# A selective scan on one core: four of sixteen states get their input through ScalarE and TensorE, GpSimd takes one more pair of products

## The chip, the cores and the metric

One of the cores of a Trainium2 chip runs the whole program. The time is the device time of one execution in microseconds (us); lower is better. TensorE does the matmuls and transposes, VectorE (DVE in the rows) the scans, ScalarE (ACT) the exponentials and copies, GpSimd (POOL) elementwise products, SyncE (SP) issues most DMAs.

## The reference, cut to what matters

A Mamba-style layer (inner width 1024, 16 states) over 4 sequences of 1024 tokens, followed by a routed transformer block on 128 chosen tokens of each sequence. All is float32. The change touches the recurrence alone, for each channel `e`, state `n` and token `t`:

```
dA[n]    = exp(delta * A[n])
state[n] = state[n] * dA[n] + (delta * u) * B[n]
y        = sum over n of state[n] * C[n]
y        = (y + D * u) * silu(z)
x        = x + tanh(g) * y      (turned: tokens by channels)
```

`delta` and `u` are channels by tokens; `B[n]` and `C[n]` are rows over the tokens, the same for all channels.

## The kernel before, in words

The program runs in stages: a projection, the **first scan** (sequences 0 and 1), routing and the transformer block for them, the **second scan** (sequences 2 and 3), routing and block again. Both scans are `scan_stage`. A scan works through 32 **units** (`UNITS`): 2 sequences, 2 halves of 512 tokens, 8 tiles of 128 channels. A unit is 128 channels by 512 tokens with 16 states, in 8 pairs. Eight units in a row share one half, and so B and C. The second half of a sequence starts its scans from `carry`; the first half ends by saving it (L820, L825, a short ScalarE copy for each pair). I call these *first-half* and *second-half* units.

For each unit `s`:
- GpSimd makes delta and `du` = delta * u of the next unit (`begin`, L592 and L596) and `x[n]` = du * B[n] for four states at once (`quad`, L607).
- ScalarE makes dA of each state with an Exp into one of four PSUM banks `pA[n % 4]` (L903). It goes pair by pair: `release(s, i - 2)` first waits until the pair that used the two banks before is done with. Between the exps it does other pieces: the softplus of the next unit, the copy of the turned gate (`copy_gate`, L798), copies for the early or late side work. I call pair `i` with what follows it on ScalarE **slot** `i`.
- VectorE scans (L969): in0 the bank, in1 `x[n]`, out in the bank, or in `hp` for the two pairs (2 and 5) whose product with C GpSimd makes (L614). The products of the other six pairs are VectorE's (L954). Its order is scan `2i`, product of pair `i-1`, scan `2i+1`. The gate multiply (L943) of the unit before stands in slot 2.
- TensorE turns each product and adds it up in `py` (4 transposes a state, `add_state`, L670), pair by pair in `SUM_ORDER`. It also runs `dt_proj` (L642), the turning of the gate (L651) and, after the gate multiply, adds x to the result in PSUM (`add_x`, L659 and L660), which ScalarE copies out (L806). One PSUM bank `pm` serves all of these in turn.

Every engine takes its instructions strictly in the order written; semaphores make it wait.

Beside this, TensorE carries other work, put after given positions of the sum order. The first scan holds a projection and convolution for the later sequences (L723, L734). The second holds an MLP of the first half's chosen tokens (`feed_forward`): 25 steps a unit, dealt out to the eight positions by `FILL`; its activations are cut into ScalarE's slots (L831 to L841) and VectorE's (L975, L982, L987), 48 VectorE instructions in all.

Behind `store(s - 1)` on SP, which waits for the finished x of the unit before, stand some loads of B and C (`load_B(c, 3)`, `load_C(c, 1)`) at a change of the half.

## Time and profile before

| | us |
|---|---|
| median of three runs | 3032.66 (3030.67 to 3033.72) |
| the profiled execution | 3037.04 |
| its span, first to last instruction | 3035.3 |
| first scan, from first to last VectorE scan | about 189 to 1026 |
| second scan | about 1432 to 2310 |

The span is 1.7 us short of the profiled execution, and that one is 4.4 us over the median. Over the whole span TensorE is busy for 79%, VectorE for 70%, GpSimd for 55% and ScalarE for 44%, but these are averages over stages of quite different kinds. In both scans VectorE is the one near full.

### The profile page before, as it was taken

The numbers are of one execution on the slowest core, as the hardware profiler recorded it, in microseconds if no ns is written. First come the engines' busy times: TensorE is split into PE (matmuls) and PEld (weight loads), VectorE is DVE, ScalarE is ACT, GpSimd is POOL, SyncE is SP. The second block draws the span as 40 slices with busy tenths as digits, with TensorE's granted clock in tenths as the row PEclk, the third lists the DMA queues.
The fourth block names the chain that finished last, engine by engine and source line by source line (L and its number), as shares of the span: only waits on it lengthen the run. The fifth ranks groups of instructions, "written<-read, shape, count | busy, mean of one in ns | idle before, by whom it ended". The sixth has DMA issues, their size and how long they took to land. (4 is left out here: it accounts for less than half of the span.)

```text
span 3035.3 us, 30042 instructions
## 1 busy us (share of the span) xinstructions
PE 2390.7 (79%) x10552; PEld 1599.8 (53%) x10552; DVE 2112.7 (70%) x2626; ACT 1339.2 (44%) x2470; POOL 1667.7 (55%) x600
## 2 busy tenths in 40 slices
PE   8848767777777546887888888888884199999998
PEld 3324444444444316653666666664552186668863
DVE  6759999999999763232999999999997633310000
ACT  5647755666555341042665555565552212410000
POOL 1169999999999400002998998999993100000000
PEclk9959999999888857998999999999997599999999
DMA  9942252342522394624235335336333453145443
GB/s 335 334 140 78 65 167 77 108 143 63 159 70 60 126 359 143 229 78 142 84 104 187 105 104 175 118 97 215 97 108 133 186 179 104 46 141 153 153 152 104
DMA packets 224869, 426.70 MB, mean 141 GB/s; under 512 B 17488, under 2 KB 101712, under 8 KB 221904
## 3 DMA queue, kind: packets, MB, share of 16 engines
q1 hardware_dynamic: 211216, 368.68, 38.6%
q10 hardware_dynamic: 12160, 51.39, 4.2%
q0 software_dynamic: 1344, 4.72, 0.4%
q8 instruction: 85, 1.39, 0.2%
q14 instruction: 64, 0.52, 0.1%
HBM read 340.84 MB, written 83.89 MB: 140 GB/s over the span
## 5 line engine op out<-in xcount | busy, mean ns | idle before, releaser
L607 POOL TENSOR_TENSOR s_x<-s_du,k_bB 128x2048 f32<-128x2048 f32 x256 | 1156.4, 4534 | 82.8 <-PE s_py L670 52.7
L903 ACT ACTIVATE s_pA<-s_delta,k_negA 128x512 f32<-128x512 f32 x1024 | 664.1, 680 | 382.3 <-DVE s_x L954 373.5
L670 PE MATMUL s_py<-k_ident,s_x 128*128 128x128 f32 x4096 | 581.8, 289 | 254.8 <-DVE s_x L954 243.6
L670 PEld LDWEIGHTS s_py<-k_ident,s_x 128*128 128x128 f32 x4096 | 506.9, 150 | 479.9 <-DVE s_x L954 331.8
L969 DVE TENSOR_TENSOR_SCAN s_pA<-s_pA,s_x 128x512 f32<-128x512 f32 x384 | 452.2, 1214 | 63.5 <-POOL s_x L607 60.7
L954 DVE TENSOR_TENSOR s_x<-s_pA,k_bC 128x1024 f32<-128x1024 f32 x384 | 464.4, 1209 | 20.6 <-DMA k_bC<-scratch_xd 20.6
L969 DVE TENSOR_TENSOR_SCAN s_pA<-s_pA,s_carry,s_x 128x512 f32<-128x512 f32 x384 | 472.8, 1276 | 3.3 <-ACT s_pA L903 1.8
L1543 PE MATMUL l_p<-l_hT,l_ring 128*128 128x256 f32 x1792 | 397.4, 381 | 2.5 <-DVE l_hT L1736 1.4
L1543 PEld LDWEIGHTS l_p<-l_hT,l_ring 128*128 128x128 f32 x1792 | 342.2, 191 | 50.4 <-issue 2.0
L614 POOL TENSOR_TENSOR s_x<-s_hp,k_bC 128x1024 f32<-128x1024 f32 x128 | 302.0, 2359 | 16.4 <-DVE s_hp L969 16.1
L1511 POOL TENSOR_TENSOR l_squares<-l_squares,l_minus_half 128x1 f32<-128x1 f32 x4 | 2.2, 556 | 508.0 <-DVE l_squares L1802 508.0
L1550 PE MATMUL l_p<-l_ring,l_hidden 128*128 128x512 f32 x512 | 220.2, 592 | 0.0
L1520 POOL DMA_INDIRECT out_dram<-l_rows,l_row_i x2 | 1.9, 953 | 331.1 <-DVE l_rows L1829 331.1
L820 ACT ACTIVATE s_carry<-s_pA 128x2 f32<-128x2 f32 x192 | 33.0, 172 | 303.2 <-DVE s_x L954 302.5
L969 DVE TENSOR_TENSOR_SCAN s_hp<-s_pA,s_carry,s_x 128x512 f32<-128x512 f32 x128 | 162.6, 1271 | 0.0
L1550 PEld LDWEIGHTS l_p<-l_ring,l_hidden 128*128 128x128 f32 x512 | 97.1, 190 | 121.1 <-issue 121.0
L1824 DVE TENSOR_TENSOR l_hidden<-l_silu,l_p 128x256 f32<-128x256 f32 x32 | 13.5, 421 | 208.4 <-PE l_p L1543 208.4
L969 DVE TENSOR_TENSOR_SCAN s_hp<-s_pA,s_x 128x512 f32<-128x512 f32 x128 | 154.5, 1207 | 0.2 <-issue 0.2
L659 PE MATMUL s_pm<-s_xt,k_ident 128*128 128x512 f32 x128 | 77.9, 693 | 96.6 <-DVE s_gy L943 90.7
L734 PE MATMUL s_p_conv<-s_raw,s_diagC 128*128 128x512 f32 x256 | 148.5, 667 | 0.9 <-ACT s_pre L884 0.9
L686 PE MATMUL s_p_gate<-s_h2T,s_ring 128*128 128x256 f32 x512 | 138.1, 407 | 0.0
L723 PE MATMUL s_p_in<-s_ctxT,s_w_in 128*128 128x512 f32 x256 | 132.7, 600 | 0.0
(194 smaller groups left out, 3086.2 us busy)
## 6 DMA issues: line engine op xcount, KB each, us to landing
k_bB<-scratch_xd SPq DMA_DIRECT2D x32, 1024.0 KB, 12.1
k_bC<-scratch_xd SPq DMA_DIRECT2D x32, 1024.0 KB, 13.3
p_xz<-in_x SPq DMA_DIRECT2D x32, 512.0 KB, 6.6
scratch_ug<-p_ug ACTq DMA_DIRECT2D x16, 1024.0 KB, 8.7
k_u<-scratch_ug SPq DMA_DIRECT2D x64, 256.0 KB, 3.6
s_gy<-scratch_ug SPq DMA_DIRECT2D x64, 256.0 KB, 4.3
s_xt<-in_x SPq DMA_DIRECT2D x64, 256.0 KB, 4.7
scratch_x<-s_xt SPq DMA_DIRECT2D x64, 256.0 KB, 3.5
```

The source lines that it names most:

```text
L607: pool.tensor_tensor(out=x[:, 4 * g:4 * g + 4], in0=du[:, s % 2:s % 2 + 1].broadcast_to([P, 4, HALF]), in1=bB[:, 4 * g:4 * g + 4], op=ALU. ...
L614: pool.tensor_tensor(out=x[:, 2 * i:2 * i + 2], in0=hp[:, POOL_PAIRS.index(i)], in1=bC[:, 2 * i:2 * i + 2], op=ALU.mult).then_inc(pool_hc, 1)
L659: nc.tensor.matmul(pm[:], ident[:], xt[:, s % 3], start=True, stop=False)
L670: last = nc.tensor.matmul(py[:, a], x[:, n, a * P:(a + 1) * P], ident[:], is_transpose=True, start=False, stop=is_last and a == HALF // P - 1)
L686: last = nc.tensor.matmul(out[:, m % 2 * ROWS:(m % 2 + 1) * ROWS], ring[:, tile % RING, c * P:(c + 1) * P], h2T[:, c], start=r % (2 * KT) ...
L723: last = nc.tensor.matmul(p_in[:], w_in[:, s % 2, i], ctxT[:, chunk(s) % 2, i], start=i == 0, stop=i == NK - 1)
L734: last = nc.tensor.matmul(p_conv[:], diagC[:, s % NE, i], raw[:, s % 2, i:i + HALF], start=i == 0, stop=i == TAPS - 1)
L903: nc.scalar.activation(pA[:, n % 4], delta[:, s % 2], ACT.Exp, scale=negA[:, s % NE, n:n + 1]).then_inc(dA_ready, 1)
L954: nc.vector.tensor_tensor(x[:, 2 * i:2 * i + 2], pA[:, j:j + 2], bC[:, 2 * i:2 * i + 2], ALU.mult).then_inc(vec_hc, 1)
L969: nc.vector.tensor_tensor_scan(out, pA[:, n % 4], x[:, n], initial, ALU.mult, ALU.add).then_inc(scanned, 1)
L1543: last = nc.tensor.matmul(out[:, 0:ROWS], w[:, c * P:(c + 1) * P], src[:, c], start=c == 0, stop=c == KT - 1)
L1550: last = nc.tensor.matmul(banks[2 * a + h][:], src[:, a * P:(a + 1) * P], w[:, h * HALF:(h + 1) * HALF], start=is_first, stop=is_last)
```

## The change: four states in turned layout, one pair more for GpSimd

Pairs 3 and 7 (states 6, 7, 14, 15) are **turned** pairs. Their `x[n]` comes another way. TensorE turns `du` of the next unit into `pm` (`turn_du`, 4 transposes), ScalarE copies it out (`copy_du`), makes du-turned times B for each of the four states in four pieces of 128 by 128, with B as a column scale (`make_state`), and TensorE turns each back into the bank `pA[n % 4]` (`turn_x`, 4 transposes a state). The exps of these pairs go to SBUF, into `x[n]`, and the scan reads the two with their parts swapped. The columns of B are loaded by `load_columns`, one element of 4 bytes at a time in both patterns.

GpSimd makes two quads of four and two of two, takes three pairs times C (1, 3 and 5; VectorE keeps five) and adds x to the result itself (`add_x`), after `quad(s + 1, 1)`. TensorE's two `add_x` matmuls and ScalarE's copy go. Positions move: the gate is turned after the first sum (before: after the fourth) and copied in slot 5 (before: 7); `FILL` still has 25 steps, nine of them now after the third sum.

The core of the diff:

```diff
-POOL_PAIRS = (2, 5)
+POOL_PAIRS = (1, 3, 5)
+TURNED = (3, 7)
-SUM_ORDER = (0, 1, 3, 2, 4, 6, 5, 7)
+SUM_ORDER = (0, 1, 2, 4, 3, 5, 6, 7)
-GATE_AT, TURN_AT, DT_AT = 2, 3, 6
-READ_AT, X2_AT, COPY_AT = 2, 5, 7
+GATE_AT, TURN_AT, DU_AT, DT_AT = 2, 0, 2, 5
+READ_AT, COPY_AT, DU_COPY_AT = 1, 5, 6
+STATE_AT = (6, 7, 4, 5)
-FILL = (2, 2, 3, 3, 3, 3, 4, 5)
+FILL = (1, 3, 9, 1, 1, 3, 3, 4)
...
+    def load_columns(self, sp, t, b, th, j, sem):
+        for k, n in enumerate((6, 7, 14, 15)):
+            at = b * ND + NR + n
+            sp.dma_start(self.BT[:, j, k], t["xd"][at:at + 1, th * HALF:(th + 1) * HALF].rearrange("n (a p) -> p (n a)", p=P),
+                         allow_slow_non_contiguous=True).then_inc(sem, 16)
...
+            def add_x(s):
+                pool.wait_ge(y_used, s + 1)
+                pool.wait_ge(xt_in[s % 3], ring3(s)[1])
+                pool.tensor_tensor(out=xt[:, s % 3], in0=xt[:, s % 3], in1=gy[:, s % 3], op=ALU.add).then_inc(x2_ready, 1)
...
+            def turn_du(s):
+                pe.wait_ge(du_ready, s + 1)
+                if s:
+                    pe.wait_ge(gate_turned, s)
+                for a in range(HALF // P):
+                    last = nc.tensor.transpose(pm[:, a * P:(a + 1) * P], du[:, s % 2, a * P:(a + 1) * P], ident[:])
+                last.then_inc(du_turned, 1)
+
+            def turn_x(s, i):
+                pe.wait_ge(scanned, NS * s + 2 * i - 2)
+                for n in (2 * i, 2 * i + 1):
+                    k = state_at(0, n) - 1
+                    pe.wait_ge(xT_ready, state_at(s, n))
+                    for a in range(HALF // P):
+                        last = nc.tensor.transpose(pA[:, n % 4, a * P:(a + 1) * P], xT[:, k, a * P:(a + 1) * P], ident[:])
+                    last.then_inc(x_turned, 1)
...
+                turn_x(s, TURNED[0])
...
+                    if i == TURNED[1] - 3:
+                        turn_x(s, TURNED[1])
                     if at == TURN_AT:
                         turn_gate(s)
+                    if at == DU_AT and s + 1 < UNITS:
+                        turn_du(s + 1)
...
+            def copy_du(s):
+                act.wait_ge(du_turned, s + 1)
+                act.wait_ge(xT_ready, NT * s)
+                nc.scalar.activation(duT[:], pm[:], ACT.Copy).then_inc(duT_ready, 1)
+
+            def make_state(s, k):
...
+                for a in range(HALF // P):
+                    last = nc.scalar.activation(xT[:, k, a * P:(a + 1) * P], duT[:, a * P:(a + 1) * P], ACT.Copy,
+                                                scale=BT[:, chunk(s) % 2, k, a:a + 1])
...
-                nc.vector.tensor_tensor_scan(out, pA[:, n % 4], x[:, n], initial, ALU.mult, ALU.add).then_inc(scanned, 1)
+                dA, added = pA[:, n % 4], x[:, n]
+                if i in TURNED:
+                    dve.wait_ge(x_turned, state_at(s, n))
+                    dA, added = added, dA
+                nc.vector.tensor_tensor_scan(out, dA, added, initial, ALU.mult, ALU.add).then_inc(scanned, 1)
```

ScalarE in the first scan, the second half of a unit. Before, from the exps of pair 4 on (L903 exps, L806 copy of x, L798 copy of the gate, L802 the scaling of u for the next unit):

```order
L903 ACTIVATE s_pA<-s_delta,k_negA 128x512 x2
L806 ACTIVATE s_xt<-s_pm 128x512
L903 ACTIVATE s_pA<-s_delta,k_negA 128x512 x4
L798 ACTIVATE s_gy<-s_pm,k_tg 128x512
L903 ACTIVATE s_pA<-s_delta,k_negA 128x512 x2
L802 ACTIVATE k_u<-k_u,k_ssm 128x512
```

And now the same stretch, slots 4 to 7 and the next unit's first exps (L966 exps, L861 `make_state`, L840 gate, L849 `copy_du`, L844 u):

```order
L966 ACTIVATE s_pA<-s_delta,k_negA 128x512 x2
L861 ACTIVATE s_xT<-s_duT,k_BT 128x128 x4
L966 ACTIVATE s_pA<-s_delta,k_negA 128x512 x2
L840 ACTIVATE s_gy<-s_pm,k_tg 128x512
L861 ACTIVATE s_xT<-s_duT,k_BT 128x128 x4
L966 ACTIVATE s_pA<-s_delta,k_negA 128x512 x2
L849 ACTIVATE s_duT<-s_pm 128x512
L861 ACTIVATE s_xT<-s_duT,k_BT 128x128 x4
L966 ACTIVATE s_x<-s_delta,k_negA 128x512 x2
L861 ACTIVATE s_xT<-s_duT,k_BT 128x128 x4
L966 ACTIVATE s_pA<-s_delta,k_negA 128x512 x2
L844 ACTIVATE k_u<-k_u,k_ssm 128x512
```

Each of slots 4 to 7 now carries one state's four pieces, and the gate's copy has moved from slot 7 to slot 5.

TensorE in the second scan, the middle of a unit. Before, from the sum of pair 1 (L670 sums, L686 MLP steps, L651 turning of the gate):

```order
L670 MATMUL s_py<-k_ident,s_x 128x128 x8
L686 MATMUL s_p_up<-s_h2T,s_ring 128x256 x2
L670 MATMUL s_py<-k_ident,s_x 128x128 x8
L686 MATMUL s_p_up<-s_h2T,s_ring 128x256 x3
L670 MATMUL s_py<-k_ident,s_x 128x128 x8
L651 MATMUL s_pm<-k_ident,s_gy 128x128 x4
L686 MATMUL s_p_up<-s_h2T,s_ring 128x256 x3
L670 MATMUL s_py<-k_ident,s_x 128x128 x8
```

And now, from the unit's start (L697 `turn_x`, L702 u, L708 sums, L680 gate, L724 MLP steps, L688 `turn_du`):

```order
L697 MATMUL s_pA<-k_ident,s_xT 128x128 x8
L702 MATMUL s_py<-k_ident,k_u 128x128 x4
L708 MATMUL s_py<-k_ident,s_x 128x128 x8
L680 MATMUL s_pm<-k_ident,s_gy 128x128 x4
L724 MATMUL s_p_up<-s_h2T,s_ring 128x256
L708 MATMUL s_py<-k_ident,s_x 128x128 x8
L724 MATMUL s_p_up<-s_h2T,s_ring 128x256 x3
L708 MATMUL s_py<-k_ident,s_x 128x128 x8
L688 MATMUL s_pm<-k_ident,s_du 128x128 x4
L724 MATMUL s_p_up<-s_h2T,s_ring 128x256 x9
L708 MATMUL s_py<-k_ident,s_x 128x128 x8
L697 MATMUL s_pA<-k_ident,s_xT 128x128 x8
```

After the third sum (pair 2) stand the four transposes of `du`, nine MLP steps, the sum of pair 4, and only then the transposes that scans 14 and 15 read.

## Rows read from the trace of the kernel before

**Rows 1.** The page, the span in 40 slices: VectorE's busy tenths.

```profile
DVE  6759999999999763232999999999997633310000
```

**Rows 2.** Timeline of VectorE, first scan, a first-half unit: start, duration, instruction.

```profile
347.15 0.67 DVE L943 TENSOR_TENSOR s_gy<-s_py,s_gy 128x512 f32<-128x512 f32 x1
...
353.34 1.21 DVE L954 TENSOR_TENSOR s_x<-s_pA,k_bC 128x1024 f32<-128x1024 f32 x1
354.46 1.22 DVE L969 TENSOR_TENSOR_SCAN s_pA<-s_pA,s_x 128x512 f32<-128x512 f32 x1
355.59 1.20 DVE L969 TENSOR_TENSOR_SCAN s_hp<-s_pA,s_x 128x512 f32<-128x512 f32 x1
...
372.47 0.67 DVE L943 TENSOR_TENSOR s_gy<-s_py,s_gy 128x512 f32<-128x512 f32 x1
```

**Rows 3.** Timeline of VectorE, second scan, scans that start from `carry`.

```profile
1777.12 1.28 DVE L969 TENSOR_TENSOR_SCAN s_pA<-s_pA,s_carry,s_x 128x512 f32<-128x512 f32 x1
1778.31 1.26 DVE L969 TENSOR_TENSOR_SCAN s_hp<-s_pA,s_carry,s_x 128x512 f32<-128x512 f32 x1
```

**Rows 4.** Timeline of GpSimd in the same unit as rows 2.

```profile
340.40 13.53 POOL L607 TENSOR_TENSOR s_x<-s_du,k_bB 128x2048 f32<-128x2048 f32 x3
353.90 2.34 POOL L614 TENSOR_TENSOR s_x<-s_hp,k_bC 128x1024 f32<-128x1024 f32 x1
356.21 1.27 POOL L592 TENSOR_TENSOR s_delta<-s_delta,s_du 128x512 f32<-128x512 f32 x1
...
358.90 4.50 POOL L607 TENSOR_TENSOR s_x<-s_du,k_bB 128x2048 f32<-128x2048 f32 x1
```

**Rows 5.** Timeline of ScalarE, first scan; in brackets idle time before and its releaser.

```profile
195.96 1.27 ACT L888 ACTIVATE s_diagC<-k_ident,s_conv 128x128 f32<-128x128 f32 x4
...
197.13 0.16 ACT L820 ACTIVATE s_carry<-s_pA 128x2 f32<-128x2 f32 x1
...
354.58 0.17 ACT L820 ACTIVATE s_carry<-s_pA 128x2 f32<-128x2 f32 x1 [1.13 <-DVE s_x L954]
354.78 1.30 ACT L903 ACTIVATE s_pA<-s_delta,k_negA 128x512 f32<-128x512 f32 x2
356.03 0.58 ACT L806 ACTIVATE s_xt<-s_pm 128x512 f32<-128x512 f32 x1
...
360.70 0.67 ACT L798 ACTIVATE s_gy<-s_pm,k_tg 128x512 f32<-128x512 f32 x1
```

**Rows 6.** Timeline of TensorE, second scan; MLP steps have two records each.

```profile
1751.86 1.04 PE L670 MATMUL s_py<-k_ident,s_x 128*128 128x128 f32 x8
1752.73 0.60 PE L651 MATMUL s_pm<-k_ident,s_gy 128*128 128x128 f32 x4
1753.17 1.46 PE L686 MATMUL s_p_up<-s_h2T,s_ring 128*128 128x256 f32 x6
1754.47 1.04 PE L670 MATMUL s_py<-k_ident,s_x 128*128 128x128 f32 x8
```

**Rows 7.** The same view, work that follows waits of TensorE.

```profile
1675.63 1.97 PE L670 MATMUL s_py<-k_ident,s_x 128*128 128x128 f32 x8 [3.45 <-DVE s_x L954]
...
1907.02 1.97 PE L670 MATMUL s_py<-k_ident,s_x 128*128 128x128 f32 x8 [4.30 <-DVE s_x L954]
...
1934.12 1.97 PE L670 MATMUL s_py<-k_ident,s_x 128*128 128x128 f32 x8 [2.97 <-DVE s_x L954]
1935.89 2.21 PE L686 MATMUL s_p_up<-s_h2T,s_ring 128*128 128x256 f32 x6
1937.93 1.04 PE L670 MATMUL s_py<-k_ident,s_x 128*128 128x128 f32 x8
...
2122.81 1.09 PE L670 MATMUL s_py<-k_ident,s_x 128*128 128x128 f32 x8 [3.03 <-DVE s_x L954]
```

**Rows 8.** Groups by line: busy us, mean ns | idle before them, releasers.

```profile
L954 DVE TENSOR_TENSOR s_x<-s_pA,k_bC 128x1024 f32<-128x1024 f32 x384 | 464.4, 1209 | 20.6 <-DMA k_bC<-scratch_xd 20.6
```

**Rows 9.** DMA issues: target and source, count, KB each, median us to landing.

```profile
s_gy<-scratch_ug SPq DMA_DIRECT2D x64, 256.0 KB, 4.3
s_xt<-in_x SPq DMA_DIRECT2D x64, 256.0 KB, 4.7
```

More of the change, by code:

```diff
@@ L356, in scan_stage @@
     act_chain, u_scaled = sem("act_chain"), sem("u_scaled")
+    du_turned, duT_ready, xT_ready, x_turned = (sem(n) for n in ("du_turned", "duT_ready", "xT_ready", "x_turned"))
+    BT_in = [sem(f"BT_in{j}") for j in range(2)]
     dt_in = [sem(f"dt_in{j}") for j in range(2)]
@@ L600, in quad @@
                     return
+                pairs = tuple(i for i in (2 * g, 2 * g + 1) if i not in TURNED)
+                many = 2 * len(pairs)
                 if g == 0:
@@ L605, in quad @@
                 if s:
-                    pool.wait_ge(summed, max(after_sum(s - 1, 2 * g), after_sum(s - 1, 2 * g + 1)))
-                pool.tensor_tensor(out=x[:, 4 * g:4 * g + 4], in0=du[:, s % 2:s % 2 + 1].broadcast_to([P, 4, HALF]),
-                                   in1=bB[:, 4 * g:4 * g + 4], op=ALU.mult).then_inc(w_ready, 1)
+                    pool.wait_ge(summed, max(after_sum(s - 1, i) for i in pairs))
+                pool.tensor_tensor(out=x[:, 4 * g:4 * g + many], in0=du[:, s % 2:s % 2 + 1].broadcast_to([P, many, HALF]),
+                                   in1=bB[:, 3 * g + g % 2:3 * g + g % 2 + many], op=ALU.mult).then_inc(w_ready, 1)
             def times_C(s, i):
@@ L738, in _ @@
             dt_proj(0)
+            turn_du(0)
             dt_proj(1)
             for s in range(UNITS):
+                turn_x(s, TURNED[0])
                 if s >= 2:
@@ L802, in scale_u @@
                 nc.scalar.activation(u[:, s % 2], u[:, s % 2], ACT.Copy, scale=ssm[:, s % NE, NS + 1:NS + 2]).then_inc(u_scaled, 1)
[L804 to L806 removed]
+            def copy_du(s):
[3 more added lines that the diff above has]
+            def make_state(s, k):
+                if s >= UNITS:
+                    return
+                if k == 0:
+                    act.wait_ge(duT_ready, s + 1)
+                    if s and s % NE == 0:
+                        act.wait_ge(BT_in[chunk(s) % 2], 64 * ((chunk(s) + 1) // 2))
+                if s:
+                    act.wait_ge(x_turned, NT * (s - 1) + k + 1)
+                for a in range(HALF // P):
+                    last = nc.scalar.activation(xT[:, k, a * P:(a + 1) * P], duT[:, a * P:(a + 1) * P], ACT.Copy,
+                                                scale=BT[:, chunk(s) % 2, k, a:a + 1])
+                last.then_inc(xT_ready, 1)
             def release(s, i):
@@ L897, in _ @@
                 act.wait_ge(act_chain, 2)
+            copy_du(0)
+            make_state(0, 0)
+            make_state(0, 1)
             for s in range(UNITS):
@@ L901, in _ @@
                     release(s, i - 2)
+                    if i in TURNED and s:
+                        act.wait_ge(summed, after_sum(s - 1, i))
                     for n in (2 * i, 2 * i + 1):
-                        nc.scalar.activation(pA[:, n % 4], delta[:, s % 2], ACT.Exp, scale=negA[:, s % NE, n:n + 1]).then_inc(dA_ready, 1)
+                        out = x[:, n] if i in TURNED else pA[:, n % 4]
+                        nc.scalar.activation(out, delta[:, s % 2], ACT.Exp, scale=negA[:, s % NE, n:n + 1]).then_inc(dA_ready, 1)
                         if fill:
@@ L924, in _ @@
                         make_taps(s)
-                    if i == X2_AT and s:
-                        copy_x2(s - 1)
                     if i == COPY_AT:
                         copy_gate(s)
+                    if i == DU_COPY_AT and s + 1 < UNITS:
+                        copy_du(s + 1)
+                    for k in range(NT):
+                        if i == STATE_AT[k]:
+                            make_state(s + (k < 2), k)
             if early:
```

62 lines of the change are left out of this document (30 added, 32 removed).

## The prediction, made before the changed kernel ran

> **What bounds the kernel now.** I read the slices of the page first. VectorE is at nine tenths or more through both scans [rows 1], so a scan's length is VectorE's length. The timelines show how tight it is. In a first-half unit scan follows scan every 1.12 to 1.13 us, a product takes 1.12, the gate multiply about 0.6, with no gap, and the unit takes 372.47 - 347.15 = 25.32 us [rows 2]; 16 x 1.125 + 6 x 1.12 + 0.6 = 25.3 says the same. A scan that starts from `carry` takes 1.19 [rows 3], so a second-half unit has 16 x 1.19 + 6.7 + 0.6 = 26.3. The surprise is GpSimd: three quads in 13.50, so 4.50 each, a product 2.31, `begin` 2.69 [rows 4]; 4 x 4.50 + 2 x 2.31 + 2.69 = 25.3. In first-half units two engines are full at once. That is what the change answers: it takes work off both.
>
> **VectorE.** One product a unit goes: -1.12 us. In 64 units that is -72 us if nothing else comes late. This is the whole possible gain; the rest asks what eats it.
>
> **GpSimd.** Two quads of 4.50, two half quads, three products, `begin`, and an add of `begin`'s size. A half quad has the elements of a product, so 2.31 or half a quad, 2.25. Sum 9.0 + 4.6 + 6.9 + 2.7 + 1.35 = 24.55 us. VectorE's own new floor is 24.2 in a first-half and 25.15 in a second-half unit. GpSimd is 0.35 over in the one and 0.6 under in the other, and the halves change every eight units, so it falls back by at most 8 x 0.35 = 2.8 us and catches up. The first scan of the next unit needs its quad some 7 us later than GpSimd makes it, by the same sums. I cost it at nothing; if that cover went, it would be 0.35 x 32 = 11 us.
>
> **ScalarE.** A state's four pieces have the form of the tap scalings: 197.13 - 195.96 = 1.17 us for four [rows 5]. Four states are 4.7 us a unit. The two 512-wide copies, one gone and one added, cancel at 0.58 [rows 5]. By its sum ScalarE fits (some 17 us of work a unit become 22), but it cannot run ahead: exps wait for their bank. So I go along the chain in slots 6 and 7. It starts when the product of pair 4 ends. ScalarE: 0.03 to start, 0.20 for saving carry (first-half units only), two exps 1.25, `copy_du` 0.58 + 0.03 because the next piece needs its result, state 1.17, another carry copy 0.10, exp of state 14 0.67, 0.03 until VectorE sees it [rows 5]: 4.06. VectorE in that time has scans 11, 12 and 13: 3 x 1.125, less the 0.09 by which the product's end overlaps the next start = 3.29 [rows 2]. It waits 0.8 us in a first-half unit. In a second-half unit it is 3.76 against 3 x 1.19 - 0.09 = 3.48: 0.3 us. The same sum over slots 4 and 5 (exps, state, carry copy, exp; 3.45 against 3.29) adds 0.15 in first-half units. So in the first scan the change is worth -1.12 + 0.95 = -0.17 in 16 units and -1.12 + 0.3 = -0.82 in 16: **-16 us** where -36 were to be had.
>
> **TensorE's order.** `turn_du(s + 1)` stands behind the third sum and needs bank `pm`, which holds the turned gate until ScalarE has copied it in slot 5. All of TensorE waits there. From the end of the product of pair 2, ScalarE needs 0.03 + 0.20 + 1.25 (exps 8, 9) + 1.17 (state 14) + 0.10 + 1.25 (exps 10, 11) + 0.67 (gate) = 4.67 us, 4.4 in second-half units [rows 5]. TensorE has summed pair 2 after 0.87 (1752.73 - 1751.86) [rows 6] and stands for 3.5 to 3.8. Then come `turn_du` 0.44, what the stage put there, the sum of pair 4 0.87, the turning of state 14 0.60 until its end, and 0.1 for two semaphores.
>
> In the first scan one projection step stands there (0.87, the size of eight transposes by the same count of columns): together 2.9 after the gate. Scan 14, by VectorE, is 7 scans and a product after pair 2's product, 8 x 1.125 - 0.09 = 8.9 us; the chain gives 4.67 + 2.9 = 7.6. It is hidden even if the clock costs 1.6 more (below).
>
> In the second scan nine MLP steps stand there, at (1754.47 - 1753.17) / 3 = 0.433 each [rows 6]: 3.9 us. The chain is 4.67 + 0.44 + 3.9 + 0.87 + 0.60 + 0.1 = 10.6 against 8.9, a wait of 1.66 us; in second-half units 10.3 against 7 x 1.19 + 1.12 - 0.09 = 9.36, a wait of 0.93. These take the place of ScalarE's waits, which end at the same scan. Net of the product: +0.54 in 16 units, -0.19 in 16: +6 us. VectorE's own MLP instructions that fall between pair 2's product and scan 14 are then free: by the new `FILL` 29 of the 48, at about 0.6 each (the gate multiply has their size), -17. ScalarE's MLP pieces in slots 4 and 5 lengthen the chain, about +8 over the stage (two softplus groups of 1.8 and four exps of 0.5). Together **-3 us**.
>
> **The clock.** Rows of work after a wait come next [rows 7]. Eight transposes after the waits of 3.45 and 4.30 us took 1.97 instead of 1.04, so the clock was at its lower level, 1.2 instead of 2.4 GHz. After 2.97 the two groups took 1.77 + 2.04 = 3.81 where rows 6 have 0.87 + 1.30: 1.64 lost. After 3.03 us, once, nothing was lost. The new wait of 3.5 to 3.8 us comes in every unit, and what follows it is the chain that scan 14 waits for. I take a loss of 1.64 in three units of four of the second scan: 24 x 1.64 = **+39 us**; the ends are 0 and 32 x 1.64 = +52, more where the low clock lasts longer. In the first scan it falls in the slack.
>
> The Trainium skill says the same of such a shape (TensorE: Matmul & The Clock Gate, HAM oscillation): bursts of matmuls with a wait for another engine between them begin each burst at the throttled clock. By that rule the loss would come in all 32 units; rows 7 have waits of this length followed by either clock.
>
> **Loads.** B's broadcasts shrink from 16 states to 12. `store(s - 1)` now waits for GpSimd's add, which ends about 1 us into the next unit; behind it stand B's last and C's second load at the six changes of the half. Before, VectorE waited 20.6 us in all for C [rows 8]. The earlier loads are asked for some 3 us sooner and are a quarter smaller in B, the later ones 1 to 3 us later. I take -3, with -15 to +25. The columns of B are 512 elements of 4 bytes each, four DMAs at each change of the half; the nearest rows are 256 KB in 128 pieces, 4.3 us, and in 512 pieces, 4.7 [rows 9]. Only those at the end of the projection stage are waited for at once: 0 to 4 x 4.7 = 19 us; against that stand 1 MB less of B. I take +2, near the 0.4 by which 512 pieces differ from 128.
>
> The Trainium skill speaks against these loads (DMA: Bandwidth & Descriptors, Rules for kernel authors): a last dimension that isn't contiguous becomes one descriptor per element. No row here has a 4-byte piece.
>
> **Sum**, against the profiled execution of 3037: -16 - 3 + 39 - 3 + 2 = +19. The median before was 3032.7, 4.4 lower, so I predict **3052 us**, slower by 0.6%: a removal that comes back as waits at scan 14.
>
> **The rivals.**
> *The clock holds.* The same waits, but TensorE stays at 2.4 GHz after them, as after the 3.03 us wait. The 39 us go: 3013. For it: the row after 3.03 us at full speed [rows 7]. Against: the new one is longer and comes beside another of about 2 us at the unit's start, where TensorE waits for scan 3.
> *VectorE is fed in time.* If ScalarE's pieces to SBUF are shorter than those I took, and its chains are under 3.3 us, no wait forms at scan 14 in the first scan; and if the gate's copy comes early enough, none in the second. Then -72 and small things: 2960 to 2975. Against it: the sums in slots 4 to 7 rest on measured gaps with at most 0.2 us of play, and the second scan's chain misses by over a microsecond.
> *The stores hold up the loads.* Slower by another way: C's second load comes 3 to 5 us too late at each of six changes, GpSimd waits for B there and loses its reserve of some 7 us. 6 x 5 = 30 on top of the forecast, 3080 or more. It decides from the point at which GpSimd's add ends more than 3 us into the next unit.
>
> **Chances.** Forecast (3035 to 3078) 0.50; the clock holds (2995 to 3035) 0.22; fed in time (2950 to 2995) 0.18; stores 0.10. A range of 2960 to 3080 leaves out the last and half of the third; the forecast's own is 3035 to 3078. A measurement of this kernel tells 0.2% from no change, 6 us. Faster by more: 0.18 + 0.18 of the 0.22 = 0.36. Within: 0.10. Slower: 0.54.
>
> **What would show it.** Right: VectorE idle before one scan a unit, the one that reads state 14 from `x`; in the first scan it is released by ScalarE, 0.9 us in first-half units and 0.3 in second-half, in the second by TensorE's L697, 1 to 3 us. TensorE idle 3.5 us before L688 in every unit, released by ScalarE's L840. Transposes of 1.9 us for eight behind it. Second-scan units of 26 to 29 us. Wrong: those waits absent or half as long, scans of 25 us a unit, or VectorE's idle time at the products (L954, for C).

## The result, and the profile of the changed kernel

The changed kernel takes **3039.68 us** (median; 3034.82 to 3047.08), the kernel before, on the same chip, 3033.67 (3026.96 to 3036.31). The ratio is 1.0024 with a 95% interval of 1.0014 to 1.0034: slower by 0.24%, some 6 to 7 us. I had predicted 3052, slower by 19. The sign was right and the time lies in the range, but the size is a third of what I gave.

The page of the changed kernel: its busy times, VectorE's slices (the line that answers to [rows 1]), and four groups by line (busy us, mean ns | idle before, releaser).

```profile
span 3034.1 us, 33855 instructions
...
PE 2431.3 (80%) x11576; PEld 1704.8 (56%) x11576; DVE 2050.8 (68%) x2562; ACT 1638.9 (54%) x3494; POOL 1622.5 (53%) x728
...
DVE  6759999999999743224998999997997633310000
...
L632 POOL TENSOR_TENSOR s_x<-s_du,k_bB 128x2048 f32<-128x2048 f32 (+1 forms) x256 | 881.6, 3455 | 98.6 <-PE s_py L708 53.3
...
L639 POOL TENSOR_TENSOR s_x<-s_hp,k_bC 128x1024 f32<-128x1024 f32 x192 | 452.6, 2369 | 51.0 <-DVE s_hp L1038 50.8
...
L861 ACT ACTIVATE s_xT<-s_duT,k_BT 128x128 f32<-128x128 f32 x1024 | 324.6, 389 | 2.1
...
L688 PE MATMUL s_pm<-k_ident,s_du 128*128 128x128 f32 x256 | 47.9, 318 | 133.9 <-ACT s_gy L840 123.2
```

The change does what it says. VectorE's busy time fell by 62 us (2112.7 to 2050.8), GpSimd's by 45 (1667.7 to 1622.5), and ScalarE took on 300. Yet the profiled execution is only 1.2 us shorter (span 3034.1 against 3035.3). VectorE's new idle time is in its waits (us in total, times, longest; over the whole program):

```profile
DVE s_pA L1038 <- PE s_pA L697: 41.5, 25, 3.6
...
DVE s_pA L1038 <- ACT s_x L966: 21.2, 38, 1.2
```

Nearly all of both stands ahead of scan 14, the first scan of the turned pair in slot 7: L697 is TensorE's turn of state 14, the exp into `s_x` is ScalarE's. The first comes in the second scan only, the second mostly in the first (15.7 us at scan 14 there, against 5.1 in the second).

To see in which stretch the time went, I take four marks from VectorE's timeline: its first scan and its last gate multiply in each of the two scan stages. Of the kernel before:

```profile
188.76 3.46 DVE L969 TENSOR_TENSOR_SCAN s_pA<-s_pA,s_x 128x512 f32<-128x512 f32 x3 [41.95 <-POOL s_x L607]
...
1028.50 0.69 DVE L943 TENSOR_TENSOR s_gy<-s_py,s_gy 128x512 f32<-128x512 f32 x1 [2.20 <-PE s_py L670]
...
1432.45 3.46 DVE L969 TENSOR_TENSOR_SCAN s_pA<-s_pA,s_x 128x512 f32<-128x512 f32 x3 [17.14 <-POOL s_x L607]
...
2312.82 0.69 DVE L943 TENSOR_TENSOR s_gy<-s_py,s_gy 128x512 f32<-128x512 f32 x1 [2.06 <-PE s_py L670]
```

And of the changed kernel:

```profile
185.76 2.35 DVE L1038 TENSOR_TENSOR_SCAN s_pA<-s_pA,s_x 128x512 f32<-128x512 f32 x2 [38.84 <-ACT s_pA L966]
...
1014.00 0.69 DVE L1008 TENSOR_TENSOR s_gy<-s_py,s_gy 128x512 f32<-128x512 f32 x1 [1.18 <-PE s_py L708]
...
1409.91 2.35 DVE L1038 TENSOR_TENSOR_SCAN s_pA<-s_pA,s_x 128x512 f32<-128x512 f32 x2 [17.50 <-ACT s_pA L966]
...
2313.99 0.69 DVE L1008 TENSOR_TENSOR s_gy<-s_py,s_gy 128x512 f32<-128x512 f32 x1 [2.06 <-PE s_py L708]
```

| stretch | before | after | difference | my forecast |
|---|---|---|---|---|
| up to the first scan | 188.8 | 185.8 | -3.0 | 0 to +2 (loads) |
| first scan stage | 839.7 | 828.2 | -11.5 | -16, and half of the -3 |
| between the stages | 404.0 | 395.9 | -8.0 | 0 |
| second scan stage | 880.4 | 904.1 | +23.7 | +36, and half of the -3 |
| behind it | 722.5 | 720.1 | -2.4 | 0 |
| sum | 3035.3 | 3034.1 | -1.2 | +19 |

(The medians differ by +6. These two profiled executions happen to lie closer to each other, by 7 us; the stretches are read against each other only within them.) So the second scan lost 11 us less than I said, the first won 6 less, and 13 us were won in places where my sum has nothing but the +2.

### The profile page after: what moved, and what is told of

Same layout as the page of the kernel before. It is cut to its first block and busy times, and to the rows that moved or that the text cites. A ratio compares the mean times of both kernels' runs of the same rounds, so it can differ in the third digit from the quotient of the medians.

```text
span 3034.1 us, 33855 instructions
## 1 busy us (share of the span) xinstructions
PE 2431.3 (80%) x11576; PEld 1704.8 (56%) x11576; DVE 2050.8 (68%) x2562; ACT 1638.9 (54%) x3494; POOL 1622.5 (53%) x728
## 2 busy tenths in 40 slices
DMA packets 237690, 418.62 MB, mean 138 GB/s; under 512 B 34384, under 2 KB 118608, under 8 KB 234704
## 5 line engine op out<-in xcount | busy, mean ns | idle before, releaser
L632 POOL TENSOR_TENSOR s_x<-s_du,k_bB 128x2048 f32<-128x2048 f32 (+1 forms) x256 | 881.6, 3455 | 98.6 <-PE s_py L708 53.3
L708 PEld LDWEIGHTS s_py<-k_ident,s_x 128*128 128x128 f32 x4096 | 501.6, 148 | 242.4 <-issue 95.8
L966 ACT ACTIVATE s_pA<-s_delta,k_negA 128x512 f32<-128x512 f32 x768 | 500.2, 681 | 221.3 <-DVE s_x L1019 216.1
L708 PE MATMUL s_py<-k_ident,s_x 128*128 128x128 f32 x4096 | 567.4, 284 | 50.1 <-POOL s_x L639 37.8
L639 POOL TENSOR_TENSOR s_x<-s_hp,k_bC 128x1024 f32<-128x1024 f32 x192 | 452.6, 2369 | 51.0 <-DVE s_hp L1038 50.8
L1019 DVE TENSOR_TENSOR s_x<-s_pA,k_bC 128x1024 f32<-128x1024 f32 x320 | 385.0, 1203 | 12.6 <-DMA k_bC<-scratch_xd 12.5
L1038 DVE TENSOR_TENSOR_SCAN s_pA<-s_pA,s_x 128x512 f32<-128x512 f32 x256 | 305.6, 1217 | 66.0 <-ACT s_pA L966 65.7
L1038 DVE TENSOR_TENSOR_SCAN s_pA<-s_pA,s_carry,s_x 128x512 f32<-128x512 f32 x256 | 320.0, 1272 | 9.2 <-ACT s_pA L966 9.0
L861 ACT ACTIVATE s_xT<-s_duT,k_BT 128x128 f32<-128x128 f32 x1024 | 324.6, 389 | 2.1
L697 PE MATMUL s_pA<-k_ident,s_xT 128*128 128x128 f32 x1024 | 150.5, 294 | 103.3 <-DVE s_hp L1038 101.3
L697 PEld LDWEIGHTS s_pA<-k_ident,s_xT 128*128 128x128 f32 x1024 | 121.8, 150 | 151.8 <-DVE s_hp L1038 148.7
L966 ACT ACTIVATE s_x<-s_delta,k_negA 128x512 f32<-128x512 f32 x256 | 169.6, 707 | 0.0
L688 PE MATMUL s_pm<-k_ident,s_du 128*128 128x128 f32 x256 | 47.9, 318 | 133.9 <-ACT s_gy L840 123.2
L1893 DVE TENSOR_TENSOR l_hidden<-l_silu,l_p 128x256 f32<-128x256 f32 x32 | 13.5, 422 | 206.1 <-PE l_p L1612 206.1
```

The lines of the kernel that those rows point to most:

```text
L632: pool.tensor_tensor(out=x[:, 4 * g:4 * g + many], in0=du[:, s % 2:s % 2 + 1].broadcast_to([P, many, HALF]), in1=bB[:, 3 * g + g % 2:3 * g ...
L639: pool.tensor_tensor(out=x[:, 2 * i:2 * i + 2], in0=hp[:, POOL_PAIRS.index(i)], in1=bC[:, 2 * i:2 * i + 2], op=ALU.mult).then_inc(pool_hc, 1)
L688: last = nc.tensor.transpose(pm[:, a * P:(a + 1) * P], du[:, s % 2, a * P:(a + 1) * P], ident[:])
L697: last = nc.tensor.transpose(pA[:, n % 4, a * P:(a + 1) * P], xT[:, k, a * P:(a + 1) * P], ident[:])
L708: last = nc.tensor.matmul(py[:, a], x[:, n, a * P:(a + 1) * P], ident[:], is_transpose=True, start=False, stop=is_last and a == HALF // P - 1)
L861: last = nc.scalar.activation(xT[:, k, a * P:(a + 1) * P], duT[:, a * P:(a + 1) * P], ACT.Copy, scale=BT[:, chunk(s) % 2, k, a:a + 1])
```

## The waits, read in one unit each

**First scan.** ScalarE in slots 6 and 7 of a first-half unit (answers to [rows 5]), from the end of VectorE's product:

```profile
380.10 0.17 ACT L877 ACTIVATE s_carry<-s_pA 128x2 f32<-128x2 f32 x1
380.31 1.30 ACT L966 ACTIVATE s_pA<-s_delta,k_negA 128x512 f32<-128x512 f32 x2
381.55 0.58 ACT L849 ACTIVATE s_duT<-s_pm 128x512 f32<-128x512 f32 x1
382.16 1.28 ACT L861 ACTIVATE s_xT<-s_duT,k_BT 128x128 f32<-128x128 f32 x4
383.34 0.19 ACT L882 ACTIVATE s_carry<-s_hp 128x2 f32<-128x2 f32 x1
383.44 1.32 ACT L966 ACTIVATE s_x<-s_delta,k_negA 128x512 f32<-128x512 f32 x2
```

VectorE in the same stretch (answers to [rows 2]):

```profile
378.87 1.20 DVE L1019 TENSOR_TENSOR s_x<-s_pA,k_bC 128x1024 f32<-128x1024 f32 x1
379.99 1.21 DVE L1038 TENSOR_TENSOR_SCAN s_hp<-s_pA,s_x 128x512 f32<-128x512 f32 x1
381.12 2.33 DVE L1038 TENSOR_TENSOR_SCAN s_pA<-s_pA,s_x 128x512 f32<-128x512 f32 x2
384.18 1.23 DVE L1038 TENSOR_TENSOR_SCAN s_pA<-s_x,s_pA 128x512 f32<-128x512 f32 x1 [0.73 <-ACT s_x L966]
```

The product ends at 380.07 and scan 14 starts at 384.18: a chain of 4.11 where I had 4.06, and a wait of 0.73 where I had 0.8. The wait is 0.73 or 0.74 in all 16 first-half units of the first scan; in second-half units it is 0.26 or 0.27 (0.3; the last unit has none). Each piece has the place and the length that I gave it.

**Second scan.** TensorE around the turn of `du` (L688), one unit (answers to [rows 6, 7]):

```profile
1731.02 0.63 PE L702 MATMUL s_py<-k_ident,k_u 128*128 128x128 f32 x4 [0.76 <-DVE s_gy L1008]
...
1735.40 1.04 PE L708 MATMUL s_py<-k_ident,s_x 128*128 128x128 f32 x8
1738.83 1.09 PE L688 MATMUL s_pm<-k_ident,s_du 128*128 128x128 f32 x4 [2.40 <-ACT s_gy L840]
```

The wait for the gate's copy is there, but it is 2.40 and not 3.5 to 3.8. The sum of pair 2 could have started when VectorE's product ended, at 1734.35. It started at 1735.40. TensorE works without a pause from L702 up to it, and L702, the turn of `u` at the unit's head, had to wait 0.76 us for the gate multiply: that is the larger part of the 1.05. ScalarE's part is as I had it: L688 starts 4.48 after that product (4.4 forecast).

What follows the wait, in four other units: full speed; a start at full speed after a longer wait, with the clock falling behind it (18 records in 5.74 us instead of 4.05); a clock at the lower level from the first row on (`down` steps stand there); and full speed again after a wait of the same length as that one:

```profile
1683.52 0.63 PE L688 MATMUL s_pm<-k_ident,s_du 128*128 128x128 f32 x4 [1.70 <-ACT s_gy L840]
1683.99 4.05 PE L724 MATMUL s_p_gate<-s_h2T,s_ring 128*128 128x256 f32 x18
1687.88 1.04 PE L708 MATMUL s_py<-k_ident,s_x 128*128 128x128 f32 x8
1688.75 1.04 PE L697 MATMUL s_pA<-k_ident,s_xT 128*128 128x128 f32 x8
...
1768.25 0.63 PE L688 MATMUL s_pm<-k_ident,s_du 128*128 128x128 f32 x4 [4.05 <-ACT s_gy L840]
1768.71 5.74 PE L724 MATMUL s_p_up<-s_h2T,s_ring 128*128 128x256 f32 x18
...
2220.00 1.08 PE L688 MATMUL s_pm<-k_ident,s_du 128*128 128x128 f32 x4 [2.40 <-ACT s_gy L840]
2220.88 1.91 PE L738 MATMUL s_p_gate<-s_ring,s_hidden 128*128 128x512 f32 x2
...
2248.23 0.63 PE L688 MATMUL s_pm<-k_ident,s_du 128*128 128x128 f32 x4 [2.41 <-ACT s_gy L840]
```

And scan 14 behind the first, the third and the fourth, on VectorE:

```profile
1689.46 1.29 DVE L1038 TENSOR_TENSOR_SCAN s_pA<-s_x,s_carry,s_pA 128x512 f32<-128x512 f32 x1 [0.44 <-PE s_pA L697]
...
2227.95 1.29 DVE L1038 TENSOR_TENSOR_SCAN s_pA<-s_x,s_carry,s_pA 128x512 f32<-128x512 f32 x1 [3.05 <-PE s_pA L697]
...
2253.71 1.29 DVE L1038 TENSOR_TENSOR_SCAN s_pA<-s_x,s_carry,s_pA 128x512 f32<-128x512 f32 x1 [0.59 <-PE s_pA L697]
```

From the start of L688 to scan 14 it takes 5.94 us at full speed with gate and up steps (my sum: 0.44 + 3.9 + 0.87 + 0.60 + 0.1 = 5.91) and 5.48 with down steps, and up to 8.04 (the unit whose L688 starts at 2273.98) when the clock was low for part of it. Four transposes in about 1.08 instead of 0.63 are the sign of the lower level (1.2 instead of 2.4 GHz). L688 itself has it in 12 of 31 units, and TensorE's waits ahead of those 12 are 2.4 to 4.24 us, 3.0 in the mean. Ahead of the others they are 2.2 in the mean, but six of them are 2.4 to 2.6, three 3.0 to 3.2, and one is 4.05.

The first four transposes don't tell all. In 16 of the 31 units the granted clock was at its lower level for part of the 5.5 us from L688 on (means of 0.56 to 0.73); in the other 15 it was 1.0 throughout. Ahead of the eight units with waits under 2.3 us it never fell; of the 14 with waits of 2.3 to 2.92 it fell in eight, of the nine with 2.99 or more in eight.

## Experiments: the two waits before scan 14

Theory T: VectorE's product is won, and it comes back as two waits at scan 14, ScalarE's in the first scan and TensorE's in the second; each can be taken away by itself with the rest of the change in place. Rivals: the time is lost to something the two waits only stand beside (the loads, GpSimd), or taking one wait away only lets the other show.

**e1: six of the nine MLP steps go one slot later, behind the turn of state 14.** Nothing else changes; the wait at L688 stays.

```diff
-FILL = (1, 3, 9, 1, 1, 3, 3, 4)
+FILL = (1, 3, 3, 7, 1, 3, 3, 4)
```

> The changed kernel with six of the nine MLP steps moved from behind the turning of du to behind the turning of states 14 and 15. Only TensorE's order in the second scan differs. If the chain gate copy, turning of du, nine steps, sum, turning of state 14 is what VectorE waits for there (41.5 us idle, released by TensorE's L697), that idle time goes nearly to 0, whatever the clock does, and ScalarE's chain (0.8 us in first-half units, 0.3 in second-half) shows in its place: about 20 to 25 us less than the changed kernel, some 3015. Rival, ScalarE's added pieces alone cost the time: no change, 3040. Rival, TensorE is simply full: the idle time moves to the next unit and the time stays at 3040.

Measured: 3006.33 us, ratio to the kernel before 0.991 (0.9885 to 0.9935), so 33 us less than the changed kernel, where I had 20 to 25. Its waits of VectorE and of TensorE:

```profile
DVE s_pA L1038 <- ACT s_x L966: 27.5, 54, 1.2
...
DVE s_pA L1038 <- PE s_pA L697: 3.0, 4, 1.1
```

```profile
PE s_pm L688 <- ACT s_gy L840: 116.1, 57, 4.2
```

The second scan stage went from 904.1 to 870.9. VectorE's waits at scan 14 fell from 46.6 to 13.8 us there, which is nearly all of it. TensorE still stands for the gate's copy, 116 us in all against 123 (68 against 78 in the second scan), and it doesn't matter: what cost time was the chain *behind* the wait.

**e2: the nine steps go ahead of the turn of `du`**, into the time in which TensorE stands.

```
+                    if fill and at == DU_AT:
+                        feed_forward(FILL_AT[-1] * s + FILL_AT[at], FILL_AT[-1] * s + FILL_AT[at + 1])
                     if at == DU_AT and s + 1 < UNITS:
                         turn_du(s + 1)
...
-                    if fill:
+                    if fill and at != DU_AT:
```

> The changed kernel with the nine MLP steps ahead of the turning of du instead of behind it. The steps then fill the time in which TensorE waited for the gate's copy. If my chain is right, the wait at L688 (some 2.5 us a unit) goes in the second scan, the low clock behind it goes with it, and the time is that of the run with six steps moved or up to 5 us less: 3010 to 3020. If the low clock came from TensorE's whole pattern and not from this wait, the second scan's mean clock stays as it is. If ScalarE's load is the cause, 3040.

Measured: 3009.1 us, 0.991 (0.9886 to 0.9934). TensorE's wait at L688 falls to 46.6 us in all (32 times) and its release of scan 14 nearly vanishes; the exp of state 14 ends last instead:

```profile
DVE s_pA L1040 <- ACT s_x L968: 38.7, 57, 2.5
```

Two different ways of shortening the same chain give the same 31 to 33 us. The mean granted clock over the second scan is 0.95 in e1 and e2, as in the kernel before, and 0.94 in the changed kernel: the gain is in what stands on the chain, hardly in a faster clock for the whole stage.

**e3: state 6 of the next unit is made in slot 7 instead of slot 6**, behind the exps that scan 14 waits for.

```
-STATE_AT = (6, 7, 4, 5)
+STATE_AT = (7, 7, 4, 5)
```

> The changed kernel with the pieces of state 6 moved from slot 6 to slot 7 on ScalarE, behind the exps of the last pair. That takes 1.17 us out of the chain product 4, exps, copy of du, state, exp 14. In the first scan the 0.73 us wait before scan 14 goes (first-half units), and 0.1 to 0.3 in second-half ones: first scan 828 to about 814 us, so 12 to 15 us less in all. In the second scan nothing or little, since TensorE's chain is the longer: 3025. Rival, the time of the first scan is set by GpSimd (24.55 us of work a unit against 24.2 for VectorE): the gain in first-half units stops at 0.8 us and GpSimd's own idle time is near 0.

Measured: 3014.78 us, 0.9932 (0.9907 to 0.9958), 25 less than the changed kernel. The first scan stage fell from 828.2 to 809.5, which is -18.7. It is more than the 12 to 15 I expected: the 15.7 us of waits at scan 14 for its exp are all gone there, and 5 us of waits for the exps of other scans with them. Where scan 14 still waits in the first scan, it is a little, for TensorE (0.8 us in all):

```profile
280.51 1.23 DVE L1038 TENSOR_TENSOR_SCAN s_pA<-s_x,s_pA 128x512 f32<-128x512 f32 x1 [0.19 <-PE s_pA L697]
```

**e4: the turn of `du` one sum later, its copy and both states in slot 7.**

```
-GATE_AT, TURN_AT, DU_AT, DT_AT = 2, 0, 2, 5
-READ_AT, COPY_AT, DU_COPY_AT = 1, 5, 6
-STATE_AT = (6, 7, 4, 5)
+GATE_AT, TURN_AT, DU_AT, DT_AT = 2, 0, 3, 5
+READ_AT, COPY_AT, DU_COPY_AT = 1, 5, 7
+STATE_AT = (7, 7, 4, 5)
```

> The changed kernel with du turned after the transposes of states 14 and 15 (one place later in the sum order), its copy and state 6 in slot 7. FILL as it is, so the nine MLP steps stand where TensorE waits for the product of pair 4. No chain is then longer than VectorE's own work: 24.2 us in first-half and 25.15 in second-half units of the first scan, about 1 us a unit less than the changed kernel there (-30 us with the small waits) and as much plus TensorE's 41 us in the second. Expected 2955 to 2980, faster than both kernels. If GpSimd is the next bound, units stop at 24.6 and the time lies near 2975. If the clock or the loads take the gain back: 3000 or more.

Measured: 2988.5 us, 0.9839 (0.9813 to 0.9865). Both waits are gone (0.3 us at the exp, 1.1 at the turn), but it is 8 us short of what I expected. Slot 7 is now fuller, and ScalarE comes late with the first exps of the next unit, as in the row below (1.34). Waits for the exps into `s_pA` add up to 26 us in the two stages, against 19 in the changed kernel and 16 in e5; that would be the 8 us, but no run takes them away by themselves.

```profile
261.87 1.23 DVE L1038 TENSOR_TENSOR_SCAN s_pA<-s_pA,s_x 128x512 f32<-128x512 f32 x1 [1.34 <-ACT s_pA L966]
```

**e5: e1 and e3 together.**

> The changed kernel with both small edits of the first batch together: state 6 made in slot 7 rather than 6, and six of the nine MLP steps moved from the TensorE slot before the turn of du x delta's state to the slot behind it. My theory: the two waits are separate terms. The first scan should be as long as with the state in slot 7 alone (about 809.5 us from first scan to last gate), the second as with the steps moved, less ScalarE's 11.8 us there: about 858 to 866 us; the whole 2972 to 2985 us, ratio 0.980 to 0.984 to the kernel before. Rival: both edits take away the same wait (whatever ends last before scan 14), so that the sum is no better than the better of the two: 3003 to 3008 us.

Measured: 2984.31 us, 0.9833 (0.9812 to 0.9854), at the upper end of what was expected; first stage 810.7, second 867.6 (858 to 866 expected). Against the changed kernel e1 gave 33, e3 25, both 55. The waits are separate terms, in two stages and on two engines, and the rival by which one hides the other falls.

## Experiments: the loads, GpSimd, and the ends of the stages

At the borders of halves GpSimd had begun to wait for B. The changed kernel, SyncE and GpSimd at one border:

```profile
372.06 0.33 SPq L466 DMA_DIRECT2D k_u<-scratch_ug  x1
...
373.97 1.57 SPq L503 DMA_DIRECT2D k_bB<-scratch_xd  x3
...
381.59 4.53 POOL L632 TENSOR_TENSOR s_x<-s_du,k_bB 128x2048 f32<-128x2048 f32 x1 [5.83 <-DMA k_bB<-scratch_xd]
```

GpSimd's waits for B sum to 42.4 us (10.8 before), while VectorE's waits for C fell from the 20.6 of [rows 8] to 12.5. The loads of B stand behind the load of `u`, and that one waits for the turn of `u` of its unit.

**e6: e5 with the first two loads of B ahead of the load of `u`** at each border.

```
+                if e == NE - 1:
+                    load_B(c, 0)
+                    load_B(c, 1)
                 load_u(s + 2)
                 load_end(s + 1)
...
                 if e == NE - 1:
-                    load_B(c, 0)
-                    load_B(c, 1)
                     load_B(c, 2)
```

> As the kernel with both edits, and at the six borders of halves the first two loads of B are issued ahead of the loads of u and of the gate on SyncE's queue. Theory: the wait of u's load for the turn of u, which the change puts later in the unit, holds up B, and GpSimd's 42 us of waits for B fall to under 20 us, the late product of pair 5 and with it ScalarE's and VectorE's wait at each border go: 5 to 12 us less than the kernel with both edits. Rival: the loads of B are limited by the transfer itself (four broadcasts and the column loads together), then the wait moves to C and the time stays within 3 us of it.

Measured: **2960.05 us**, 0.9751 (0.9732 to 0.977): 24 less than e5, twice what I expected, and the best of all versions, 2.5% under the kernel before. GpSimd's group now reads:

```profile
L633 POOL TENSOR_TENSOR s_x<-s_du,k_bB 128x2048 f32<-128x2048 f32 (+1 forms) x256 | 882.2, 3459 | 51.5 <-PE s_py L709 44.5 <-DMA k_bB<-scratch_xd 2.9
```

**e8: the same edit in the changed kernel alone. b2: the same edit in the kernel before.** These ask how much of the borders the change itself brought.

> The changed kernel with one edit: at the six borders of halves the first two loads of B are issued ahead of the loads of u and of the gate on SyncE's queue. With the two other edits in place this gave 24 us (first scan 10.8 us shorter, second 13.8). Theory: the late loads of B at the borders are a term of the change of its own, some 4 us at each of six borders, independent of the waits before scan 14: 3010 to 3020 us, ratio about 0.993. Rival: in the changed kernel as it stands the lateness is partly given back by the waits for the turned state, which end later anyway: within 8 us of the changed kernel, 3028 to 3036 us.

> The kernel before with the same edit of the order of loads alone. Theory: before the change the turn of u comes earlier in a unit and GpSimd waits for B only 10.8 us in all, so the edit is worth at most a third of what it is with the change: 3028 to 3035 us, 0 to 8 us less. Rival (the loads at the borders are as late in the kernel before, their wait only shows elsewhere): 15 to 25 us less, 3010 to 3020 us; then the borders are no cost of the change.

Measured: e8 3026.66 us, 0.9984 (0.9973 to 0.9994), against the 1.0024 of the changed kernel 0.40% or 12 us less. b2 3022.48 us, 0.9969 (0.9959 to 0.9978), 9 less than the kernel before. Both fall between what theory and rival gave. The late loads were a fault of the kernel before already. The change added about 3 us to it, which is within the uncertainty of the two ratios (each 0.1% to either side). And most of GpSimd's 42 us of waits for B cost nothing: in e8 they fall to 2.5, the time falls by 12, and GpSimd's waits for TensorE's sums rise from 53.3 to 67.8. The same edit is worth 24 only once the other two waits are gone.

**e7: e5 with four of the six reloads of the B columns left out**, so that later halves are made with the columns of an earlier one.

```
-                keep.load_columns(sp, t, b, th, c % 2, BT_in[c % 2])
+                if c < 2:
+                    keep.load_columns(sp, t, b, th, c % 2, BT_in[c % 2])
...
-                    if s and s % NE == 0:
+                    if s and s % NE == 0 and chunk(s) < 2:
                         act.wait_ge(BT_in[chunk(s) % 2], 64 * ((chunk(s) + 1) // 2))
```

The second edit leaves out ScalarE's waits for the loads that are gone.

> As the kernel with both edits, but four of the six reloads of the B columns at the borders of halves are left out (the states of the later halves are made with the columns of an earlier one). Theory: the column loads, although 6.7 us each to land and in 4-byte pieces, cost little: 0 to 3 us. Rival (their packets hold up the broadcasts of B and C and SyncE's queue): 6 to 12 us less, and GpSimd's waits for B fall by half.

Measured: 2988.23 us, 0.9842 (0.982 to 0.9864), no less than e5's 2984.31, and GpSimd's waits for B are 32.5 us against e5's 23.4, not half. The 6 to 12 us of the rival are not there: the column loads at the borders have no cost that these runs can see, though each takes long for its 2 KB, as the issues of the changed kernel show (KB each, median us to landing):

```profile
k_BT<-scratch_xd SPq DMA_DIRECT2D x32, 2.0 KB, 6.7
```

**b1: the kernel before with three pairs times C on GpSimd and no turned states.**

```diff
-POOL_PAIRS = (2, 5)
+POOL_PAIRS = (1, 3, 5)
...
-SUM_ORDER = (0, 1, 3, 2, 4, 6, 5, 7)
+SUM_ORDER = (0, 2, 1, 4, 3, 6, 5, 7)
...
-                times_C(s, 2)
+                times_C(s, 1)
                 if s + 1 < UNITS:
                     begin(s + 1)
+                times_C(s, 3)
```

> The kernel before with the GpSimd half of the change alone: three pairs times C on GpSimd, no state turned and no addition of x there. GpSimd then has some 27.6 us of work for each unit, against VectorE's 24.2: by that it is the bound, first-half units last 27.6 instead of 25.3 and second-half units 27.6 instead of 26.2, about 32 x 2.3 + 32 x 1.3 = +115 us, 3140 to 3155 us (ratio 1.035 to 1.04). Rival: GpSimd has room, and the time falls by the 1.1 us a unit of VectorE: 2965 to 2990 us.

Measured: 3083.48 us, 1.0147 (1.0123 to 1.0171). GpSimd is the bound: VectorE waits 141.3 us for it, 47 times; the starts of the two stages are among them, and 82 us lie inside the scans. GpSimd itself has no idle time before its products with C. So VectorE's product can only be moved if GpSimd gives something up, which is what the four turned states are for. The size was wrong, 47 and not 115 us: I took first-scan units for both stages. The first stage grew by 37.6 (to 877.3), but units of the second were 880.4 / 32 = 27.5 us long already, and 27.6 changes them little (+9.2).

```profile
DVE s_pA L970 <- POOL s_x L607: 141.3, 47, 42.0
```

**b3: the kernel before, with only the last unit's x added by GpSimd** in each stage.

```diff
+            pool.wait_ge(y_used, UNITS)
...
+            pool.tensor_tensor(out=xt[:, (UNITS - 1) % 3], in0=xt[:, (UNITS - 1) % 3], in1=gy[:, (UNITS - 1) % 3], op=ALU.add).then_inc(x2_ready, 1)
...
-            add_x(UNITS - 1)
...
-            copy_x2(UNITS - 1)
```

> The kernel before with one piece of the change: only the last unit of each of the two scans has x added by GpSimd instead of by two matmuls and a ScalarE copy. Theory: the tail of a scan stage, from the last gate multiply to the next stage's first instruction, shrinks from 12.7 us to about 9.4 as in the changed kernel, in both scans, and the scans themselves stay as they are: 6 to 7 us in all, ratio 0.9977 to 0.998. Rival: the tail is set by something else (the last convolution of the first stage, the store), which ends as late: under 1.5 us in the trace, and no measurable difference.

Measured: 3032.74 us, 0.9988 (0.9977 to 0.9999), 3.6 less. In the first stage its last gate multiply stands at 1033.07 and the next stage starts at 1042.45:

```profile
1033.07 0.69 DVE L945 TENSOR_TENSOR s_gy<-s_py,s_gy 128x512 f32<-128x512 f32 x1 [2.20 <-PE s_py L674]
...
1033.84 1.26 POOL L634 TENSOR_TENSOR s_xt<-s_xt,s_gy 128x512 f32<-128x512 f32 x1 [7.64 <-DVE s_gy L945]
...
1042.45 0.10 POOL L1124 MEMSET r_minus_half<- 128x8 f32 x1 [7.35 <-POOLq L1847]
```

That is 9.4 us, as in the changed kernel, against 12.7 before, where the two matmuls that add x stand behind the last convolution on TensorE. In the second stage no convolution stands there and the tail shrinks by 1.3 only (9.7 to 8.4); I had expected 3.3 in both. The two tails give 4.6 us where the ratio gives 3.6, with an interval that almost reaches zero.

## Why the prediction was wrong, point by point

- **VectorE**, -1.12 a unit: right.
- **GpSimd at nothing**: right away from the borders; b1 shows that without the turned states it would have been the bound.
- **ScalarE's chain in slots 6 and 7**: right in place and size, 4.11 for 4.06 and waits of 0.73 and 0.26 for 0.8 and 0.3, and e3 takes them away. The first scan stage came to -11.5 instead of -17.5 all the same. Second-half units are 25.44 us (25.38 forecast). First-half units are 25.37 in the first sequence and 25.24 in the second, instead of 25.15: behind a wait the next scan follows at 1.14 where I had 1.125, and in the first sequence, where ScalarE also makes the taps, the exp for scan 6 comes 0.02 late and that scan starts 1.24 behind the one before. That is some 3 us in 32 units. About 3 more stand at the three borders of halves: the unit at the second of them is 3.1 us longer than before (31.38 against 28.27), that at the third 2.2 shorter, and neither was in my sum by itself. VectorE's scans with swapped parts take no longer where nothing waits (1.11 and 1.13 in unit 18).
- **TensorE's order**: right in mechanism and in the chain behind L688 (5.94 for 5.91), confirmed by e1 and e2. The wait at L688 was mis-sized, 2.5 us on the average of the second scan instead of 3.5 to 3.8. I took TensorE to be ready when the product of pair 2 ends, and left out that the turn of `u` waits for the gate multiply. The chain itself doesn't change by that. It is 0.46 shorter in the ten units with `down` steps, though, and that I had not seen either.
- **The clock, the step that failed most in the sum.** I took 1.64 us in 24 units, +39. Of the 25 units in which TensorE released scan 14, 15 had a granted clock of 0.71 to 0.80 from L688 to scan 14 and a chain longer than the full-speed 5.94 or 5.48, by 1.8 on average: 27 us in sum, 25 of it as VectorE's idle time. The other ten had a clock of 1.0. The price of one loss was right, the number of units was not. Two more kernels here have the same order on TensorE in the second scan: e3 has 13 such units and 25 us, e8 17 and 32. The likely reason is the mis-sized wait: behind waits of 2.99 us or more the clock fell in eight of nine units, and I had 3.5 to 3.8 in all of them, but only nine were so long. No run changes this wait alone, so this stays argued.
- **The rest of the second scan.** Adding the rest, the waits at scan 14 there were 47 us (41.5 for TensorE, 5.1 for ScalarE) where my terms together had 72. Against these 25 stand 9 us of longer waits elsewhere in the stage, most of them for exps ahead of other scans (13.5 us against 4.3 before), and VectorE's work fell by 32 instead of 36. For both I had nothing. So the stage came out 11 us under the forecast and not 25; that the errors cancel in part is luck.
- **Loads**: the -3 can't be seen (the units at the three borders of the first scan are together 1.4 us longer than before, those of the second 0.3), and it is a net of two larger things, B later and C earlier, and the rival on stores named the right place: GpSimd did wait 5 to 8 us at a border. The load of `u`, not the store, stood in the way, and its price in the changed kernel was 12 us, of which about 9 were there before.
- **Outside the scans** I had nothing but the +2, and there are -13 us. Of these -3.3 and -1.3 are the tails (b3), a step I saw as an edit of ScalarE and TensorE "in a unit" and never followed to the last unit, where nothing hides it. The first scan stage starts 3.0 us earlier, and the stage ahead of the second one, from its first instruction to the first scan, is 4.8 us shorter (386.5 against 391.3). It is no accident of one execution: in the nine kernels with the turned states these are 185.8 to 188.6 and 386.5 to 388.7, in the four without them 188.8 to 191.1 and 389.0 to 391.9. Both places have one megabyte less of B to load for the scan, and the last of these loads lands 4 to 6 us earlier in the two traces. That this is the cause is argued from it, not shown by a run. The last 1 us is in the stages at the end.

In sum: -11 in the second scan, -15 outside the scans against the +2, and +6 in the first scan turn +19 into -1 in the profiled executions; the medians have +6.

The Trainium skill's case of matmul bursts that each start throttled (TensorE: Matmul & The Clock Gate, HAM oscillation) has waits of some 3 to 5 us for a DMA between them. The trace agrees in part where the waits are of that length, 2.99 us or more: five of nine began at the lower level and three more fell to it within 5.5 us. Most waits at L688 were shorter, and there the lower level followed 8 of 22. The prediction applied that case to all 32 units.

The Trainium skill's warning that a last dimension which isn't contiguous becomes one descriptor per element (DMA: Bandwidth & Descriptors, Rules for kernel authors) agrees with the page of the profile: packets under 512 B rose from 17488 to 34384, and four loads of 512 elements at eight borders and starts are 16384 of them. Its price was small here, as e7 shows.

## What to carry to other kernels

When work leaves the engine that bounds a kernel, write down for the slot that scan, product or matmul waits on the whole chain of the *other* engines from their last release to it; here two such chains were 0.3 to 0.7 and 0.4 to 3.6 us too long, and two numbers in a table (which slot makes a state, which slot holds the filler steps) turned +0.2% into -1.7%, and the order of a few loads that into -2.5%. Filler work on TensorE belongs behind what another engine waits for, or ahead of the wait, never between the wait and that. And follow every moved step to the last unit of a loop as well: what is hidden in the body stands bare at the end.
